# The last token group's QKV products, in twelve items beside the first attention batch

## What is computed

```python
qkv = x @ w_qkv                                  # 1024 -> 32*32 + 2*8*32 columns
xq, xk = _apply_rope(xq), _apply_rope(xk)        # 32 query heads, 8 key/value heads of 32
scores = where(causal, xq @ keys.T * scale, -inf)
x = _layernorm(x + softmax(scores) @ values @ w_o)
x = _layernorm(x + cross_attention(x, ctx))      # Wq, Wk
x = _layernorm(x + x @ dequant(qweight, lut4).T + bias)
```

## Time and profile before

| | us |
|---|---|
| three runs, median (lowest to highest) | 1329.45 (1328.9 to 1330.63) |
| the profiled execution | 1327.51 |
| its span, first to last instruction | 1325.7 |
| PE busy in the span | 1279.0 (96%) |
| DVE busy | 896.8 (68%) |
| ACT busy | 531.1 (40%) |
| POOL busy | 476.8 (36%) |
| DMA, mean rate over the span | 128 GB/s |

### The profile page before, as it was taken

How to read it: one execution, slowest core, us unless ns; L and a number is a source line. 1 busy time by engine, 2 the same in 40 slices (tenths; PEclk the granted TensorE clock), 3 DMA queues, 4 the chain that set the end, 5 groups by cost and what they waited for, 6 DMA issues and landing times.

```text
span 1325.7 us, 24773 instructions
## 1 busy us (share of the span) xinstructions
PE 1279.0 (96%) x7990; PEld 1040.6 (78%) x7990; DVE 896.8 (68%) x2496; ACT 531.1 (40%) x1587; POOL 476.8 (36%) x403
## 2 busy tenths in 40 slices
PE   8989899997899999999999999999999999999998
PEld 6878788885677777777777788788888888788886
DVE  7987888437888778787875886345353535556665
ACT  4220212128877777777672112333343423100000
POOL 3511121235556556465562000234545350212221
PEclk9999899997899999999999999999999999999999
DMA  7253535339443433443434123314141337322221
GB/s 272 89 185 114 176 109 189 136 136 278 148 119 119 137 120 112 129 137 114 127 112 143 51 66 109 114 64 175 56 148 66 134 121 298 115 95 95 95 78 65
DMA packets 132593, 170.60 MB, mean 129 GB/s; under 512 B 36368, under 2 KB 94736, under 8 KB 131856
## 3 DMA queue, kind: packets, MB, share of 16 engines
q1 hardware_dynamic: 132496, 169.47, 38.4%
HBM read 112.80 MB, written 56.62 MB: 128 GB/s over the span
## 4 chain that ended last, share of the span: by engine, by line
PE 66%; issue 14%; DVE 10%; POOL 4%; ACT 2%; DMA 2%; SPq 2%; DVEq 0%; POOLq 0%; ACTq 0%
PE bank L625 13%; PE bank L627 13%; PE bank L626 13%; PE bank L773 10%; PE bank L717 6%; PE bank L702 3%; POOL x2b L1855 3%; PE bank L744 2%; PE bank L674 1%; DVE pick L1391 1%; PE bank L748 1%; DVE bank L1444 1%; DVE pick L1402 1%; ACT prob L1094 1%; PE bank L888 1%
## 5 line engine op out<-in xcount | busy, mean ns | idle before, releaser
L1782 POOL TENSOR_TENSOR prob<-prob,rinv 128x512 f32<-128x512 f32 x192 | 206.5, 1076 | 177.2 <-DVE rinv L1452 177.1
L1094 ACT ACTIVATE prob<-bank,nmax 128x256 f32<-128x256 f32 (+1 forms) x512 | 210.9, 426 | 95.3 <-DVE nmax L1444 81.5
L1444 DVE CUSTOM_DVE_ANT_0 bank<-bank,mask 128x256 f32<-128x256 f32 (+1 forms) x512 | 169.2, 383 | 29.2 <-PE bank L702 21.5
L625 PE MATMUL bank<-xc_hi,w_hi 128*128 128x512 f32 x320 | 128.4, 401 | 15.3 <-DVE xc_lo L1308 15.2
L717 PE MATMUL bank<-ident,prob 128*128 128x128 f32 x768 | 127.2, 290 | 6.7 <-POOL prob L1782 5.0
L626 PE MATMUL bank<-xc_lo,w_hi 128*128 128x512 f32 x320 | 126.9, 397 | 0.0
L627 PE MATMUL bank<-xc_hi,w_lo 128*128 128x512 f32 x320 | 126.7, 396 | 0.0
L717 PEld LDWEIGHTS bank<-ident,prob 128*128 128x128 f32 x768 | 87.5, 145 | 43.5 <-issue 18.1
L702 PE MATMUL bank<-k,q 96*128 96x256 f32 (+1 forms) x512 | 106.4, 312 | 7.3 <-DMA vv<-v_scr 5.5
L1094 ACT ACTIVATION_READ_ACCUMULATOR prob<-bank,nmax 128x1 f32 x512 | 108.0, 211 | 0.0
L773 PE MATMUL bank<-wo_hi,att_hi 128*128 128x512 f32 x256 | 103.9, 406 | 0.0
(11 more groups left out here) (177 smaller groups left out, 3058.7 us busy)
## 6 DMA issues: line engine op xcount, KB each, us to landing
q<-qk_scr SPq DMA_DIRECT2D x192, 128.0 KB, 2.3
qk_scr<-rot SPq DMA_DIRECT2D x80, 256.0 KB, 2.5
x_st<-x_scr SPq DMA_DIRECT2D x32, 512.0 KB, 3.7
xc_in<-x_cols SPq DMA_DIRECT2D x32, 256.0 KB, 5.0
y<-x SPq DMA_DIRECT2D x16, 512.0 KB, 3.5
x_scr<-y SPq DMA_DIRECT2D x16, 512.0 KB, 2.7
cx_in<-ctx_in SPq DMA_DIRECT2D x16, 512.0 KB, 5.1
x_scr<-x_st SPq DMA_DIRECT2D x16, 512.0 KB, 3.3
```

The lines of the kernel that those rows point to most:

```text
L625: nc.tensor.matmul(o, l_hi, r_hi, start=first, stop=False)
L1094: mm = nc.scalar.activation(prob[:, k % 4, i * keys:(i + 1) * keys], SBANK[pos][:, i * keys:(i + 1) * keys], ACT.Exp, bias=nmax[:, k % 4, ...
L1444: mm = nc.vector.tensor_tensor_reduce(part, part, mask[:, 2 * P - keys:2 * P], 1.0, BIGGEST, ALU.add, ALU.min, nmax[:, k % 4, i:i + 1])
L1782: nc.gpsimd.tensor_tensor(pr, pr, rinv[:, k % 4, 0:n].unsqueeze(2).to_broadcast([P, n, keys]), ALU.mult)\
```

## The change

The last group is taken out of stage 1 (`FULL` = 3 groups remain) and its products are computed inside batch 0 of stage 2: 12 items of 48 matmuls with 256 columns, two of values and ten of pairs (one pair of one sequence, both halves in one bank), which alternate between banks 6 and 7. PE runs 28 or 29 of these 576 matmuls in each of the steps 0 to 19 (`fill`). The 20 decode parts all lie in the three groups now, two of them at the last place; block 4's transposes are in steps 3 and 4. SP loads x for the next group before it stores pair 3, and ACT and DVE split it earlier. The item's rope, copies, low parts and stores stand in the steps of batch 0 (`ITEM_DONE`). Loads of w_o, w_q and y1 move to later places.

```diff
+        early = [sb("bits", [P, BITS, D], I32), pick_a, sb("pick_b", [P, D], I32), sb("pick_c", [P, D], I32)]
+        with nc.sbuf_tensor("rot_last", [P, 2, 4, SEQ], F32) as rot_last:
             pass
+        early += [sb("pick_t", [P, D], I32), sb("pick_e", [P, D], I32)]
...
+        ORDER = [(g, c) for g in range(FULL) for c in range(PAIRS + 1)]
+        PARTS_OF = {(g, c): ((1, 1, 0, 1, 1, 1), (1, 2, 1, 1, 1, 1), (1, 2, 1, 1, 1, 2))[g][c] for g, c in ORDER}
...
+        ITEMS = [("values", 0, j) for j in range(2)] + [("pair", c, e) for c in (0, 1, 4, 2, 3) for e in range(2)]
+        ITEM_MMS = 6 * KT
+        FILL_STEPS = 20
+        ITEM_DONE = {-(-(i + 1) * FILL_STEPS // len(ITEMS)): i for i in range(len(ITEMS))}
+        TURN_LAST = {3: 0, 4: 1}
-        WO_STEPS = {14 + kt: kt for kt in range(KT)}
+        WO_STEPS = {(0, 16): 0, (0, 17): 1, (0, 18): 2, (0, 19): 3, (0, 21): 4, (0, 22): 5, (1, 0): 6, (1, 1): 7}
...
+            for g in range(FULL):
+                for c in range(PAIRS - 2):
                     decode_loads((g, c))
                     store_pair(g, c)
+                for kt in range(KT):
+                    load_x(g + 1, kt)
+                decode_loads((g, PAIRS - 2))
+                store_pair(g, PAIRS - 2)
                 decode_loads((g, PAIRS - 1))
...
+            sp.wait_ge(fps_ready, 2 * EARLY)
+            load_unit(0, 3, False)
+            store_f(EARLY - 1)
+            load_wo((2, 3))
             load_unit(0, 4)
+            store_item(2)
+            store_item(3)
             load_unit(0, 5)
+            store_item(4)
+            sp.wait_ge(b_done, item_pair(5) + 1)
+            load_wo((4, 5))
             load_unit(0, 6)
+            store_item(5)
+            load_wo((6, 7))
+            store_item(6)
+            sp.wait_ge(b_done, item_pair(7) + 1)
             load_unit(0, 7)
+            load_wo((0, 1))
+            store_item(7)
+            store_item(8)
+            load_unit(1, 0)
+            store_item(9)
+            store_item(10)
+            load_unit(1, 1)
+            store_item(11)
             def stage2_batch(b, age, last):
                 load_unit(b, 2)
+                if age == 1:
+                    load_wq(range(4))
                 load_unit(b, 3)
+                if age == 1:
+                    load_wq(range(4, KT))
+                    for slot in range(2):
+                        sp.wait_ge(r_stored[slot], 64 * ((LAST_PAIRS + 1 - slot) // 2))
+                    sp.wait_ge(v_stored, 32 * GROUPS)
+                    for st in range(2):
+                        load_y1(0, st)
...
+            def fill(k):
+                if k >= FILL_STEPS:
+                    return
+                for at in range(len(ITEMS) * ITEM_MMS * k // FILL_STEPS, len(ITEMS) * ITEM_MMS * (k + 1) // FILL_STEPS):
+                    i, m = at // ITEM_MMS, at % ITEM_MMS
+                    if i == 0 and m == 0:
+                        pe.wait_ge(f_lo_ready, 2 * (EARLY - 1))
+                    if i == 0 and m % 6 == 0:
+                        pe.wait_ge(x_lo_ready, KT * FULL + kt + 1)
+                    if i in (2, 3) and m == 0:
+                        pe.wait_ge(v_copied, 2 * FULL + i - 1)
+                    if i > 3 and m == 0:
+                        pe.wait_ge(r_ready, item_pair(i - 2) + 1)
...
                 for k in range(SUB):
                     scores(b, k)
+                    if age == 0 and TURN_LAST.get(k) == 0:
+                        turn_last(0)
+                    if age == 0:
+                        fill(k)
+                    if age == 0 and TURN_LAST.get(k) == 1:
+                        turn_last(1)
                     project_step(b, k, age)
...
             for g, c in ORDER:
+                if c == PAIRS - 1:
+                    for kt in range(4):
+                        x_high(g + 1, kt)
                 if c < PAIRS:
+                    rope_high(PAIRS * g + c)
                 else:
+                    for kt in range(4, KT):
+                        x_high(g + 1, kt)
                     values_out(g, 0)
...
+                if n == PAIRS * FULL:
+                    dve.wait_ge(f_stored, 32 * EARLY)
+                wait(dve, r_stored[n % 2], 64 * (n // 2))
...
+                steps = [go for part in PARTS[PART_END[g, c] - PARTS_OF[g, c]:PART_END[g, c]] for go in part]
+                for i, go in enumerate(steps):
+                    if c == PAIRS - 1 and i in (0, 2):
+                        for kt in range(2 * i, 2 * i + 4):
+                            x_low(g + 1, kt)
+                    go()
...
+                    if age == 0 and ITEM_DONE.get(k, 0) > 1:
+                        rope_item(ITEM_DONE[k])
+                    if age == 0 and k in TURN_LAST:
+                        f_low(EARLY - 1, (OBANK, OBANK), (TURN_LAST[k],))
...
                     scale_probs(b, k)
+                    if age == 0 and ITEM_DONE.get(k - 1, 0) > 1:
+                        rope_low(item_pair(ITEM_DONE[k - 1]))
```

More of the change, by code:

```diff
@@ L1029, in tile_high, with f_high @@
                     copy(dst[:, 4 * h:4 * h + 4, :].rearrange("p k s -> p (k s)"), banks[h][:, :]).then_inc(done, 1)
-            def f_high(b, banks=FBANK):
-                for h in range(2):
+            def f_high(b, banks=FBANK, halves=(0, 1)):
+                for h in halves:
                     act.wait_ge(fps_ready, 2 * b + h + 1)
@@ L1082, in _ @@
                     values_out(g, 1)
-            for slot in range(2):
-                act.wait_ge(r_stored[slot], 64 * PAIRS * GROUPS // 2)
             def exponent(b, k):
@@ L1108, in att_high @@
             def att_high(b, pair):
+                if isinstance(b, int) and b == 0 and pair == 0:
+                    for slot in range(2):
+                        act.wait_ge(r_stored[slot], 64 * ((PAIRS * FULL + 1 - slot) // 2))
                 wait(act, att_ready, KVH * b + 2 * pair + 2)
@@ L1316, in tile_low, with f_low @@
                 mm.then_inc(done, 1)
-            def f_low(b, banks=FBANK):
-                for h in range(2):
+            def f_low(b, banks=FBANK, halves=(0, 1)):
+                for h in halves:
                     dve.wait_ge(f_hi_ready, 2 * b + h + 1)
@@ L1346, in rope_pair @@
-                times(odd[:, :], odd, 1).then_inc(b_turned, 1)
-                dve.wait_ge(b_turned, n + 1)
-                nc.vector.tensor_tensor(rot[:, slot, 0, :], rot[:, slot, 0, :], odd[:, :], ALU.subtract)
-                nc.vector.tensor_tensor(rot[:, slot, 2, :], rot[:, slot, 2, :], even[:, :], ALU.add).then_inc(r_ready, 1)
+                    return nc.vector.tensor_tensor(pair(o), pair(i), tab[:, ty + t, :].unsqueeze(1).to_broadcast([P, seqs, SEQ]),
+                                                   ALU.mult)
```

188 lines of the change are left out of this document (97 added, 91 removed).

## The result

The changed kernel takes 1346.0 us (median of four runs, 1344.0 to 1351.0) against 1329.2 before in the same session: ratio 1.0134, interval 1.0107 to 1.016, so 16.8 us slower. The forecast was 8.3 us slower, 1337.7: sign right, a microsecond inside the upper end of the range (1347), but only half the size. The profiled execution took 1346.8 us with a span of 1345.0, 19.3 more than the span before.

The account below looks back on a forecast made before the run. PE was taken as the bound, busy 96% of the span, so only its waits and low clock could pay. 41.6 - 33.8 + 0.5 = +8.3 us on 1329.45 gave 1337.7 us, range 1320 to 1347.

Parts of the forecast that it names:

- Part 1: Between token groups: earlier x loads and splits remove 9.5 us of xc_lo waits and 3.8 of low clock, 13.3 us gained.
- Part 2: Last group's matmuls become 576 of 256 columns inside the first attention batch: matmuls cost 3.2 us more; change S - 33.8 us.
- S: What PE loses to waits and low clock in the new stretch up to the first projection: 41.6 us, ends 16 to 58.
- (a): Start of the first batch: PE waits 10.7 us behind DVE's decode chain, plus 2.0 low clock: 12.7 us (8 to 16).
- (b): Steps 5 and 6: item 2's rope waits for the last f store, issued behind unit 3: 3.0 us (0 to 5).
- (f): Item 9's rope waits for a store behind unit 7 and two w_o loads: 7.0 us with low clock (3 to 10).
- rival 3: Stores land behind w_o and unit packets, 5.6 us instead of 2.5, and batch 1 waits for units: 1350 us; chance 0.12.
- (g): Steps from 20 to the first projection: item 11's rope waits for item 9's store behind unit (1,0): 7.5 us (3 to 10).
- Part 4: Moved DMAs: wq and y1 loads shifted to the second batch cost 0.5 us (0 to 4); other moved work 0 while covered.
- Rival 1: Stores are not late, so item waits and tail shrink and S is 20.7: 12.6 us faster, 1316.9 us; chance 0.28.
- Rival 2: The two errors cancel, time unchanged within 2.7 us, S between 30.6 and 36; chance 0.10.
- Rival 4: Between groups DVE reaches x_lo late, so 5 us of the 13.3 stay: 1343 us; chance 0.08.

Follow-up runs that it names:

- e5: Changed kernel, but in the last group before the attention ACT does rope and f copies before splitting x, and DVE three decode steps before f_low: 1340.5 us.
- e14: e13 plus six repeated, waited-for products in each of the last two items' ropes, 4.6 us more DVE work: 1323.2 us.
- e15: e13 with the ropes of items 10 and 11 computing only 16 of 256 columns in four of six operations; output not the reference's: 1313.2 us.
- e13: Four-slot kernel with spread w_q loads, plus w_o splits moved to earlier steps and the second batch: 1314.9 us.
- e4: Changed kernel with w_o splits moved: two to steps 11 and 13, two kept in 16 and 17, four into the second batch: 1347.7 us.
- e2: Changed kernel with SP issuing stores of items and f ahead of the unit loads they stood behind: 1330.65 us.
- e3: Changed kernel with four rope slots over rot for items 2 to 9, and rot_last only for items 10 and 11: 1320.9 us.
- e6: Changed kernel with the edits of e2, e3, e4 and e5 together: 1311.9 us.
- e1: Kernel before, still with four groups in stage 1, plus only the earlier x loads and splits: 1317.4 us, ratio 0.9913.
- e9_dummy: e3 with 24 idle 256-column matmuls in each of five steps behind the fill, results unused: 1327.9 us.

## Why the forecast was right in sign and half in size

**Part 1** held. Priced at 13.3 us, 12.2 measured alone. In the changed kernel the values of group 2 begin at 199.5 (198.7 forecast); the wait for xc_lo between groups is gone, and a wait of 1.3 us for DVE's rope, the margin called "nothing to spare", took its place.

**Part 2, the work.** The matmuls kept their price. Three of the fill, at clock 1.00 (start, us, instruction):

```profile
242.10 0.28 PE L756 MATMUL bank<-xc_hi,w_lo 128*128 128x256 f32 x1
242.22 0.28 PE L756 MATMUL bank<-xc_hi,w_hi 128*128 128x256 f32 x1
242.34 0.28 PE L756 MATMUL bank<-xc_lo,w_hi 128*128 128x256 f32 x1
```

0.12 us apart, as the earlier trace rows. The 109 ns that the Trainium skill's formula gave (TensorE: Matmul & The Clock Gate, Back-to-back issue gap; it is there the gap of an isolated matmul) would have been 6 us too little here as well.

**S, term by term.** The stretch from the last values matmul (211.0) to the first projection (365.2) took 154.2 us, 100.0 of work and 54.2 of S, where 41.6 was forecast. The terms:

- (a) wait 10.0 us, 10.7 forecast. The chain was the forecast one. The end of the decode, the first maxima behind it, and PE's first scores matmul after the wait:

```profile
231.97 1.29 DVE L1507 COPY_PREDICATED pick_a<-bits,pick_b 128x1024 int32<-128x1024 int32 x1
233.16 0.43 DVE L1548 CUSTOM_DVE_ANT_0 bank<-bank,mask 128x256 f32<-128x256 f32 x1
235.23 0.76 PE L783 MATMUL bank<-k,q 96*128 96x256 f32 x2 [9.97 <-ACT prob L1179]
```

  The decode ended at 233.2, 232.2 forecast. (What the walk calls "three more choices" are one choice and two leaves; its 3.0 us fit these.) The idle time of 6.1 us that the walk has in it (ACT splitting x tiles first) was what e5 then took back.
- xc_lo, 2.2 us in the first fill; the walk had 1.3, the sum had none of it.
- (b) 6.25 us, 3.0 forecast, still the right mechanism: the f store behind unit 3. The walk started SP at the end of step 4. SP was then still held, and its queue shows by what:

```profile
238.39 9.01 SPq L425 DMA_DIRECT2D v_scr<-v_st  x2
247.44 0.47 SPq L453 DMA_DIRECT2D q<-qk_scr  x1
...
251.36 0.43 SPq L458 DMA_DIRECT2D vv<-v_scr  x1
251.84 0.47 SPq L432 DMA_DIRECT2D f_scr<-pick_t  x1
252.34 0.58 SPq L432 DMA_DIRECT2D f_scr<-pick_e  x1
```

  Unit 3's issues take 4.4 us, not 3.2, and the stores leave at 251.8. The two stores of values (v_scr), 13.0 us of waiting for ACT's copies in all, stood in front of everything; I had not put them in the walk.
- (c) 1.60 and 0.40 us, 1.7 and 0.7 forecast. (d) 1.15, 2.3 forecast. (e) 4.26, 4.7 forecast.
- (f) 6.88 us, 5.0 forecast. Unit 7's issues began at 320.35, the stores of item 7 behind it at 324.55, and DVE's rope at 331.2: 6.7 us for issue and landing where 1.8 + 2.5 had been counted. For the landing I had taken the median of the kernel before; the stores issued there took 3.6 to 4.9 us, and rival 3's 5.6 was nearer here. The median of all stores of items was 2.1, so rival 3 was wrong for the rest.
- Low clock between 211.0 and 342.8: 131.8 us less 93.1 of work and 32.9 of waits leaves 5.8 for it, and the three estimates of 2.0 sum to 6.0.
- (g) 15.5 us above the 6.9 of PE's work, 7.5 forecast. This is the step that failed: the stretch behind the fill took 22.4 us, not 14.4.

The waits at the items are 3.1 too few in the forecast (17.4 against 20.5), the stretch behind the fill is 8.0 too short, xc_lo 2.2; (a) and the clock are 0.9 too long. That is the 12.6 by which S was short, but for a wait of 0.2. The stretch also began 0.7 us late, and the first projection came at 365.2 instead of 351.9. From there on the changed kernel was 2.3 us better than forecast: 11.0 us in the profiled execution, 8.5 in the medians.

**What was wrong in (g).** It followed one chain: unit (1,0), the store of item 9, DVE's rope, the next maxima, and 5.4 us from these to the first projection. The first part of it held. From SP's first issue of unit (1,0) at 343.45 the rope of item 11 began 7.6 us later (7.3 forecast), and the maxima behind it at 354.30, 10.9 us later (9.6 forecast), because a w_o split of 1.2 us stood between. From these maxima to the first projection at 365.2 are 10.9 us, not 5.4: that is 5.5 of the 8.0 that (g) was short. The 5.4 came from the start of the first batch before, where no such work lay beside it. Here DVE has two more w_o splits and two attention splits in that time and is busy 11.7 us from 353.2 to 365.2, and POOL has the low parts of items 10 and 11 between the probabilities that PE waits for (start, us, instruction, idle before):

```profile
355.28 1.04 POOL L1889 TENSOR_TENSOR prob<-prob,rinv 128x512 f32<-128x512 f32 x1 [4.83 <-DVE rinv L1556]
356.28 0.73 POOL L1868 TENSOR_TENSOR rot_last<-rot_last 128x256 f32<-128x256 f32 x1
356.96 0.73 POOL L1869 TENSOR_TENSOR rot_last<-rot_last 128x256 f32<-128x256 f32 x1
357.65 2.02 POOL L1889 TENSOR_TENSOR prob<-prob,rinv 128x512 f32<-128x512 f32 x1
359.64 0.72 POOL L1868 TENSOR_TENSOR rot_last<-rot_last 128x256 f32<-128x256 f32 x1
360.32 1.18 POOL L1869 TENSOR_TENSOR rot_last<-rot_last 128x256 f32<-128x256 f32 x1
361.46 4.49 POOL L1889 TENSOR_TENSOR prob<-prob,rinv 128x512 f32<-128x512 f32 x3
```

The chain that the profile follows back from the end runs on POOL from here to 363.5, 8.2 us, 3.2 of it low parts of items, which (g) doesn't count. What the runs show is that DVE's uncovered work lengthens the stretch (e14 and e15 in full, e13 4.8 us for 5.8, e4 3.8 us for 5.8, as the store's chain takes over) and that the store is 1.8 us of it (e2). How the last 10 us divide between DVE and POOL is not shown.

Part 4 had said it and then not used it: "0, as long as PE's fill of 3.46 us covers them". In the steps where the splits stand, the fill doesn't. The price given for lost cover, 1.07 us on ACT, was for the wrong engine; DVE pays 1.22 where nothing disturbs it, and the four in the stretch took 1.42 on average. The rows could have told it. In batch 1 DVE is busy 40.06 of 50 us at 2.09 us a step, 1.67 us a step, so six steps are 10.0; with two ropes of 2.2 and four splits of 1.22 that is 19.3 us of DVE's work, where 6.9 of PE's stood in the sum and 19.1 were measured. The Trainium skill gives the DVE price too: its formula for a float32 addition of two tensors, (N + 151)/0.96 ns (VectorE: DVE Perf Modes, The TRN2 errata), makes 1.22 us of the 1024 columns of a w_o split and 0.42 of a 256-column rope product, an estimate for our subtraction and multiplication. The rows of the changed kernel agree (1222 ns, the median of all eight splits, and 416 and 423).

**Part 4.** 0.5 us forecast; from the first projection on, the changed kernel takes 979.8 us and the one before 981.6, 1.8 less. In it stands a wait of 3.8 us for vv that wasn't there before, so the moved w_q loads do cost something; what gives more than that back I don't know. In every kernel that reached the second batch earlier, the cost came out: 4.0 us in e5, 5.0 in e3, 5.1 in e2, 6.6 in e6, 7.0 in e4.

**The rivals.** Rival 1 (stores not late, 1316.9) is what e3 built: 1320.9. It had 5 us for (b) to (f), where 2.0 were left, and 3 us for the tail, where 15.1 stood (22.0 less 6.9); the stretch from the first projection on gave some of it back. Rival 2, no change, lay 14 us off. The times of rivals 3 and 4, 1350 and 1343, lay nearer to 1346.0 than the forecast did, by luck: neither has the mechanism. Rival 3 had the right direction for (f), and batch 1 did wait for a unit, but not with the size of its price. Rival 4 can be ruled out: no wait for xc_lo stands between the groups of the changed kernel, and e1 gained 12.2 of 13.3 us. As to the order of SP's queue, its cost is larger than the sum of its waits: e2 took 13.1 us of waits away and gained 15.4.

## What to carry to other kernels

When work that covers a stretch is moved or ends early, price every engine in the bare steps by its whole busy time there, not by the one chain that comes to mind. The largest sum is what the stretch can't go below (DVE's was 85% of it in the changed kernel, 96% in e3); then look which engine hands over last, and what stands in its queue between the pieces that the others wait for. In a queue that works in order, put stores that free a buffer ahead of loads that have slack, and walk that queue from the instruction it is really standing at. A part that pays alone (the earlier x loads, 12 us) is worth shipping without its companion; the companion paid only after its slots, its queue order and its splits were changed too.

## What the runs showed of the hardware

In e9_dummy idle matmuls brought TensorE's granted clock from 0.50 to 1.00, from the lower of its two levels (1.2 GHz) to the upper (2.4 GHz), and the kernel became 7 us slower: the filler itself was then the pace, with PE busy 25.5 of 28.5 us. What a full clock alone would be worth there isn't shown. The Trainium skill (TensorE: Matmul & The Clock Gate, HAM oscillation — how this bites in real kernels) advises, for thin matmuls that wait for loads, an order of work that keeps the engine from idling. Useful work does that here (e3 ran the fill at 1.00 from 250 to 317 us); filler did not pay.

Where DVE and POOL worked at the same time, both took longer over the same instruction. A w_o split took 1.22 us at 347.07 and 353.17, where POOL was idle, but 1.50 and 1.75 at 357.27 and 360.83, where it was busy; POOL's scaling of 512 columns took 1.04 us before that and 2.02 beside the first of the two.

In e3 a 32 KB vv load, issued behind eight 512 KB loads of w_q and two of y1, landed 10.4 us after its issue, against 3.3 for the fastest of its kind in the same stretch.
